# A hand-written order of stages for each engine ahead of the first scan

## What is computed (the reference, cut)

```python
# layer 1: selective scan, 16 states (the part that the change touches)
x_proj = x @ W_xproj.T                       # 64 + 16 + 16 columns: dtp, B, C
dt = softplus(dtp @ W_dt.T + b_dt)           # 256 columns
h = exp(dt * A) * h + dt * B * x             # per time step, feature and state
y = einsum(h, C) + D * x
# layer 2: sign(layernorm(x)*gamma+beta) @ sign(W - mean(W)).T, + bias, * alpha
# layer 3: a second selective scan (rank 128 in place of 64)
# layer 4: mixture of 16 experts, top 2, and 2 shared experts
```

## Time and profile before

| | us |
|---|---|
| median of 3 runs | 688.4 (686.29 to 689.64) |
| profiled execution, its own time | 688.48 |
| its span in the trace | 686.7 |
| PE busy over the span | 623.1 (91%) |
| DVE busy | 528.3 (77%) |
| ACT busy | 503.8 (73%) |
| POOL busy | 419.1 (61%) |

### The profile page before, as it was taken

One profiled execution on the slowest core, in us unless ns is written; L12 is line 12 of the kernel. 1 busy time (PEld: TensorE's weight loads), 2 busy tenths in 40 slices (PEclk: granted clock), 3 DMA queues, 4 the chain that ended last, 5 costly groups with the idle time before them and its releaser, 6 DMA issues.

```text
span 686.7 us, 12401 instructions
## 1 busy us (share of the span) xinstructions
PE 623.1 (91%) x4334; PEld 533.4 (78%) x4337; DVE 528.3 (77%) x900; ACT 503.8 (73%) x1164; POOL 419.1 (61%) x256
## 2 busy tenths in 40 slices
PE   4779999999992778899999999989999999999994
PEld 2369999999992533799999999977677677777673
DVE  6698999999998899799899999967822644444346
ACT  2999999999974866999999999794544562222244
POOL 0037999999999003189999999980774233333400
PEclk9989999999997799999999999999999999999998
DMA  6022454545450000135445544471232233333183
GB/s 192 4 80 89 161 149 146 149 143 155 138 144 0 1 2 5 70 118 156 154 146 154 147 156 144 127 225 42 78 108 100 77 108 106 101 107 107 63 259 123
DMA packets 57575, 77.83 MB, mean 113 GB/s; under 512 B 8112, under 2 KB 38480, under 8 KB 57520
## 3 DMA queue, kind: packets, MB, share of 16 engines
q1 hardware_dynamic: 53728, 66.75, 32.1%
q0 software_dynamic: 3792, 10.36, 4.2%
HBM read 58.21 MB, written 18.87 MB: 112 GB/s over the span
## 4 chain that ended last, share of the span: by engine, by line
PE 64%; DVE 15%; ACT 8%; POOL 8%; issue 3%; DMA 1%; DVEq 0%; ACTq 0%; POOLq 0%
PE both L1311 16%; PE both L1391 12%; PE bank L1340 12%; POOL arena L1118 7%; PE both L1313 5%; PE bank L1399 3%; PE bank L1400 3%; DVE st L411 2%; DVE arena L645 2%; PE bank L1332 2%; PE bank L1493 1%; DVE residual L572 1%; DVE tok_a L497 1%; PE bank L1452 1%; PE bank L1454 1%
## 5 line engine op out<-in xcount | busy, mean ns | idle before, releaser
L1118 POOL TENSOR_TENSOR arena<-arena,rings 128x1024 f32<-128x1024 f32 x126 | 296.6, 2378 | 17.9 <-DVE arena L645 14.0
L1311 PE MATMUL both<-rings,tok_a 128*128 128x128 f32 x1280 | 182.4, 276 | 3.2 <-DVE arena L645 2.8
L1311 PEld LDWEIGHTS both<-rings,tok_a 128*128 128x128 f32 x1280 | 163.8, 192 | 4.7 <-issue 3.5
L645 DVE TENSOR_TENSOR_SCAN arena<-rings,both 128x1024 f32<-128x1024 f32 x64 | 145.3, 2279 | 13.0 <-PE both L1313 7.8
L645 DVE TENSOR_TENSOR_SCAN arena<-late,both 128x1024 f32<-128x1024 f32 x62 | 140.7, 2278 | 6.7 <-PE both L1313 1.5
L1340 PE MATMUL bank<-ident,arena 128*128 128x128 f32 x1024 | 133.0, 273 | 2.8 <-POOL arena L1118 1.4
L1340 PEld LDWEIGHTS bank<-ident,arena 128*128 128x128 f32 x1024 | 115.7, 141 | 4.2 <-POOL arena L1118 1.9
L1003 ACT ACTIVATE rings<-ident,b_tok 128x128 f32<-128x128 f32 x320 | 106.4, 393 | 0.3
L1159 POOL DMA_INDIRECT y_tok<-rings,dest x47 | 45.1, 959 | 84.9 <-DVE rings L798 84.6
L1003 ACT ACTIVATE rings<-tok_a,b_tok 128x256 f32<-128x256 f32 x192 | 89.5, 499 | 0.0
L1313 PE MATMUL both<-ident,rings 128*128 128x128 f32 x384 | 83.9, 273 | 0.0
(11 more groups left out here) (230 smaller groups left out, 976.3 us busy)
## 6 DMA issues: line engine op xcount, KB each, us to landing
rings<-c_rows SPq DMA_DIRECT2D x128, 256.0 KB, 3.4
w_sb<-w SPq DMA_DIRECT2D x18, 352.0 KB, 4.2
x_sorted<-zeros SPq DMA_DIRECT2D x47, 128.0 KB, 3.4
rings<-x_sorted SPq DMA_DIRECT2D x47, 128.0 KB, 2.0
arena<-w SPq DMA_DIRECT2D x2, 2048.0 KB, 12.9
residual<-x SPq DMA_DIRECT2D x4, 512.0 KB, 5.9
tok_a<-y_tok SPq DMA_DIRECT2D x4, 512.0 KB, 7.2
w_sb<-y_tok SPq DMA_DIRECT2D x4, 512.0 KB, 8.0
```

The source lines that it names most:

```text
L645: dve.tensor_tensor_scan(h_s, decay_s.rearrange("p h t -> p (h t)"), both[s % B_RING][:, :], 0.0, ALU.mult, ALU.add).then_inc(h_ready, 1)
L1118: pool.tensor_tensor(h_both, h_both, c_row, ALU.mult).then_inc(hc_ready, 1)
L1311: pe.matmul(o, tok_a[:, c, h * P:(h + 1) * P], v_ring[:, s % V_RING, j, 0:P], start=True, stop=True)
```

## The change

1. Each engine gets its own hand-written list ahead of the first scan: `vector_first`, `scalar_first`, `tensor_first`. GpSimd does its four `dt` products in order, as it did.
2. VectorE takes all four statistics ahead of the norms of batches 1, 2 and 3. The treatment of the second layer's weights (`ffn_weights`) becomes a stage `ffn` behind `err` 1. ScalarE's exponent of `a_sb` becomes a stage `a_exp`.
3. For batches 0 and 1 the maxima are taken by VectorE (stage `relu`, with a semaphore `relu_first`) and not by ScalarE's Relu. TensorE's `pre` 1 and 2 and VectorE's `err` 0 and 1 wait for it.
4. TensorE turns the identity 28 times as soon as the identity has landed, ahead of `turn` 0.
5. `u_turn` 0 stands ahead of `pre` 3 and B's columns on TensorE; the decay factors stand ahead of `log` 3 on ScalarE. `decays` is split in two by name; in `scalar_middle` both stand one behind the other, so nothing moves there.

The rows below are from the programs' lists of instructions: line, operation, output<-inputs, shape, and xN for N in a row. They tell the order, not times.

The diff, without the list of semaphores and with the second half of the lists as they are:

```diff
-        into_ssm = ["x_stat", "x_norm", "turn", "proj", "pre", "err", "log", "b_cols", "dt", "u_turn"]
+        vector_first = [
+            ("x_stat", 0), ("x_norm", 0), ("x_stat", 1), ("x_stat", 2), ("x_stat", 3), ("x_norm", 1), ("x_norm", 2), ("relu", 0),
+            ("err", 0), ("x_norm", 3), ("relu", 1), ("dt", 0), ("err", 1), ("ffn", 0), ("dt", 1), ("err", 2), ("b_cols", 1),
+            ("dt", 2), ("err", 3), ("dt", 3)]
+
+        scalar_first = [
+            ("x_stat", 0), ("turn", 0), ("x_stat", 1), ("x_stat", 2), ("proj", 0), ("x_stat", 3), ("pre", 0), ("turn", 1),
+            ("a_exp", 0), ("proj", 1), ("log", 0), ("turn", 2), ("pre", 1), ("proj", 2), ("turn", 3), ("log", 1), ("pre", 2),
+            ("b_cols", 0), ("proj", 3), ("u_turn", 0), ("log", 2), ("pre", 3), ("decays", 0), ("decays", 1), ("log", 3),
+            ("u_turn", 1), ("u_turn", 2), ("u_turn", 3)]
+
+        tensor_first = [
+            ("turn", 0), ("proj", 0), ("pre", 0), ("turn", 1), ("proj", 1), ("turn", 2), ("pre", 1), ("proj", 2), ("turn", 3),
+            ("pre", 2), ("proj", 3), ("dt", 0), ("u_turn", 0), ("pre", 3), ("b_cols", 1), ("u_turn", 1), ("u_turn", 2)]
...
+                elif name == "ffn":
+                    ffn_weights()
                 elif name == "err":
 
-                    if k == 0:
-                        ffn_weights()
-                    elif k == Q + 2:
+                    if k == Q + 2:
                         keep()
...
                     if l:
                         dve.wait_ge(relu_ready, (q + 1) * H)
+                    elif q < 2:
+                        dve.wait_ge(relu_first, (q + 1) * H)
...
                         dve.tensor_scalar(dtT[:, h, t], bank[2 + h][:, :], bdt_sb[l][:, h:h + 1], 0.0, ALU.add, ALU.max)\
-                           .then_inc(relu_ready, 1)
+                           .then_inc(relu_ready if l else relu_first, 1)
...
-            for name, q in in_turn(into_ssm, range(Q)):
+            for name, q in vector_first:
                 stage(name, q, 0)
...
+                elif name == "a_exp":
+                    for i in range(2):
+                        act.wait_ge(ld_ssm[i], 32)
+                        act.activation(a_sb[i][:, :, :], a_sb[i][:, :, :], ACT.Exp).then_inc(a_exp_ready, 1)
                 elif name == "b_cols":
                     if l == 0 and q == 0:
-                        for i in range(2):
-                            act.wait_ge(ld_ssm[i], 32)
-                            act.activation(a_sb[i][:, :, :], a_sb[i][:, :, :], ACT.Exp).then_inc(a_exp_ready, 1)
                         act.wait_ge(fsign_in, 2)
...
                         act.wait_ge(pre_ready, k * H + h + 1)
-                        if l == 0:
+                        if l == 0 and q >= 2:
                             act.activation(dtT[:, h, t], bank[2 + h][:, :], ACT.Relu, bias=bdt_sb[l][:, h:h + 1])
...
-                    if q == 1 and l == 0:
-                        for s in range(0, ABAR_RING, 2):
-                            decays(l, s)
...
                 elif name == "decays":
-                    for s in range(0, ABAR_RING, 2):
-                        decays(l, s)
+                    decays(l, 2 * q)
...
-            for name, q in in_turn(into_ssm, range(Q)):
+            for name, q in scalar_first:
                 stage(name, q, 0)
...
-            for name, q in in_turn(into_ssm, range(Q)):
-                stage(name, q, 0)
+            for q in range(Q):
+                stage("dt", q, 0)
...
                     if k > Q:
                         pe.wait_ge(relu_ready, q * H)
+                    elif k in (1, 2):
+                        pe.wait_ge(relu_first, k * H)
...
             pe.wait_ge(ld_ident, 16)
-            for name, q in in_turn(into_ssm, range(Q)):
-                if (name, q) != ("u_turn", Q - 1):
-                    stage(name, q, 0)
+            stay_busy(28, bank[4])
+            for name, q in tensor_first:
+                stage(name, q, 0)
```

More of the change, by code:

```diff
@@ L197, in sandwich_kernel @@
         shift_ready, bias_ready, minus_ready = sem("shift_ready"), sem("bias_ready"), sem("minus_ready")
-        g_first, relu_ready = sem("g_first"), sem("relu_ready")
+        g_first, relu_ready, relu_first = sem("g_first"), sem("relu_ready"), sem("relu_first")
         g_normed, x_scaled, rows_normed = sem("g_normed"), sem("x_scaled"), sem("rows_normed")
@@ L255, in sandwich_kernel @@
             ("exp", 0), ("bc", 1), ("turn", 2), ("pre", 1), ("log", 0), ("exp", 1), ("proj", 2), ("turn", 3), ("log", 1), ("bc", 2),
-            ("pre", 2), ("exp", 2), ("proj", 3), ("log", 2), ("bc", 3), ("pre", 3), ("u_turn", 0), ("exp", 3), ("decays", 1),
+            ("pre", 2), ("exp", 2), ("proj", 3), ("log", 2), ("bc", 3), ("pre", 3), ("u_turn", 0), ("exp", 3), ("decays", 0), ("decays", 1),
             ("log", 3), ("u_turn", 1), ("u_turn", 2), ("u_turn", 3)]
@@ L1538, in diagonals @@
     return 2 if 1 <= batch_state(s)[1] <= 2 * CQ else 3
-def in_turn(stages, batches=range(Q - 1, -1, -1)):
-    for step in range(len(stages) + Q - 1):
-        for q in batches:
-            if 0 <= step - q < len(stages):
-                yield stages[step - q], q
 class Tile:
```

## The result

| us | before | after |
|---|---|---|
| median, beside each other on one chip | 689.02 (4 runs, 686.29 to 691.25) | 695.74 (4 runs, 693.06 to 700.36) |
| profiled execution; its span | 688.48; 686.7 | 694.72; 692.9 |
| ScalarE's first input part | 49.64 | 52.99 |
| first scan step of VectorE | 53.17 | 58.06 |
| first scan step to the last of the first scan | 154.34 | 154.35 |

What follows compares the result with a forecast made beforehand. Bound: ScalarE, almost gapless from `pre` 0 to the first input part at 49.64. Terms -3.65 - 2.3 + 0.96 + 5.35 = +0.35, then +1.5 + 0.93 for the clock, gave +2.8: 691.2 us, 8 in 10 for 687.0 to 693.6.

Steps and rivals of the forecast that it cites:

- `pre` 0 at 15.7: First stretch: with statistics ahead of norms and 28 turns, `pre` 0 starts at 15.7, not 19.34: -3.65 us.
- Rival 3: Start of TensorE: the 28 turns don't raise the clock, `pre` 0 from 18, 2.2 later; 693.4 us, chance 0.08.
- ScalarE's new waits: ScalarE from `pre` 0 to the input part: waits sum to 6.7 us against 1.35 before, +5.35.
- The 0.25 at the signs: ScalarE at the signs of the weights, 34.6: TensorE's turn and the hand-overs cost 0.25 us.
- the 0.3 in `pre` 0: ScalarE's first wait, between the two halves of `pre` 0: 0.3 us.
- Rival 1: `pre` 0 to input part: 32.5 us, as tight as between the layers; input part 48.2, 687.0 us, chance 0.16.
- The prediction's two bounds for the waits: ScalarE's waits behind 15.7: under 6.3 us the tight order decides; under 3.5, input part 46.2, gain over 0.5%.
- VectorE held by GpSimd at w: `err` 1 on VectorE: its w meets GpSimd's `dt` product, +1.05 us, or nothing if VectorE goes first.
- The clock's term: TensorE's low clock after gaps 30.7 to 35.4 (+1.5, bounds 0 and 2.4) and 44.5 to 49.4 (+0.93, 0 and 1.9).
- What stands behind that runs as before: Behind the first input part, 49.64: nothing changes, so a microsecond there is a microsecond at the end.
- Rival 2: TensorE's two new gaps: the clock stays high through both, +0.35 us in all; 688.8 us, chance 0.16.
- The marks that it named: Signs in the trace: `pre` 0 about 15.7, waits at `proj` 1, `log` 1, `pre` 3, 22 turns nearly 3.9, input part 51 to 52.5.

Runs made afterwards that it cites:

- e2: The changed kernel without the 28 turns of the identity at the start; 699.25 us, 1.0102 of the kernel before.
- e1: The changed kernel with 15, 38 and 42 turns of the identity in TensorE's three gaps; 689.83 us, 1.0013 of the kernel before.
- e4: The changed kernel with `err` 1 ahead of `dt` 0 and `err` 2 ahead of `dt` 1 on VectorE; 691.54 us, 1.0012 of the kernel before.
- f2: The changed kernel with norm 1 ahead of statistics 3 on VectorE, `turn` 1 ahead of `pre` 0 on ScalarE and TensorE; 700.38 us, 1.0068 of before.
- g4: The changed kernel measured once more, unaltered; 693.88 us, 1.0102 of the kernel before.
- g1_stats_row: The kernel before with only VectorE's statistics of batches 1 to 3 ahead of their norms; 687.18 us, 0.9991 of the kernel before.
- f1_before_28: The kernel before with 28 turns of the identity at its start and nothing else; 696.4 us, 1.0006 of the kernel before.
- g3_third_gap: The changed kernel with 42 turns of the identity behind `u_turn` 1, in the third gap alone; 691.1 us, 1.0036 of the kernel before.
- g2: The changed kernel with reordered lists, 20 and 14 turns behind `u_turn` 0 and 1, and 34 more between the layers; 683.92 us, 0.9919 of before.
- f3: The changed kernel with the order of e4 and 15, 20 and 42 turns of the identity in TensorE's gaps; 696.25 us, 1.0007 of the kernel before.
- the second set: Second of three sets of follow-up runs, on one chip beside the kernel before (median 695.29 us there); f1_before_28, f2 and f3 belong to it.

## Why the prediction was wrong

It had the sign, and a time of 691.2 with a range up to 693.6; the measured 695.74 lies outside. At the first scan step it had +2.78 (0.35, 1.5 and 0.93), and the trace has +4.89. Of the 4.5 us between 691.2 and 695.74 these are 2.1, which alone would give 693.3, still in the range; 1.3 came behind the first scan step, 0.6 because the kernel before measured 689.02 and not 688.4 this time, and 0.5 lie between spans and medians. By its own steps:

- *`pre` 0 at 15.7.* 16.05. The 28 turns took 5.57, past the 5 us of its high end; the clock rose in them and `proj` 0 took 1.93. Rival 3 did not come, and e2 shows how it would have looked (`pre` 0 at 17.75 without the turns; it had 18). The Trainium skill, "TensorE: Matmul & The Clock Gate", section "What's actually happening", has activity release the high level; `turn` 0 at 1.04 with the turns and 1.94 without agrees.
- *ScalarE's new waits, +5.35 and with them +0.35 in all.* Right in place, and nearly in size. With the clock held high (e1) they are 1.88 (2.0 predicted), 2.52 (2.6), 0.73 (0.55) and 0.79 (1.0), and the first scan step stands 0.45 behind that of before. The 0.25 at the signs and the 0.3 in `pre` 0 did not come. e4 and f2 take single waits away, and each moves part of its time to a later wait.
- *Rival 1, the new order as tight as between the layers* (32.5 us from `pre` 0 to the input part). It took 36.9, and 33.8 in e1 with the clock high, where the waits behind `pre` 0 sum to 5.9: so 3.1 of the 4.4 us to this rival were the clock's. The prediction's two bounds for the waits don't fit its own sum, in which the input part is at 43.3 plus the waits: 48.2 needs 4.9 and not 6.3, and 46.2 needs 2.9 and not 3.5.
- *VectorE held by GpSimd at w.* Right: three of three, 1.82 to 1.84 for two.
- *The clock's term, 1.5 + 0.93 = 2.43: this is the step that failed.* Held against e1_awake it cost 4.64 in both profiled executions of the changed kernel. In the first, the gap of 1.86 us ahead of `proj` 1 counted too, 1.54, where the prediction listed two gaps only, "30.7 to 35.4 and [...] about 44.5 to 49.4"; its own words on the earlier trace rows ("gaps of 2 us and weak work") had room for it, since by its own times TensorE, done with `turn` 1, stands idle for ScalarE's Exp and copies up to 19.2. The two it listed cost 1.56 (1.5 predicted) and 1.54 (0.93): the third stretch lasted 6.83 us, into the first products of the scan, where the one between the layers, from which the 0.93 was taken, lasted 3.4 in the kernel before. In the second (g4) the gap at `proj` 1 cost nothing and the listed ones 2.65 and 2.00, both above their bounds of 2.4 and 1.9. So a missing gap is one way in which the term was too small, and too low a price for the listed ones the other; the 22 turns, forecast at nearly 3.9, took 3.13 and 4.23. For the first execution the difference to the forecast at the first scan step, 4.89 - 2.78 = 2.11, is 1.54 for the stretch left out, 0.06 and 0.61 for the other two, 0.35 for `pre` 0, and 0.45 less for the waits.
- *"What stands behind that runs as before."* The scan does (154.34 and 154.35). Between the layers 1.18 more went. No line there was changed, and the same code took from 83.53 (g1_stats_row) to 85.06 (f1_before_28) in two kernels that keep the old lists there and ahead of it nearly so. Both executions of the changed kernel lie high (84.84; 82.09 with the shorter meeting told last, so 84.95 without), but g3_third_gap, with the same lists, has 80.59 with that meeting, so 83.45 without. So the executions alone spread as widely, and a share of the change in it isn't shown. The last 0.5 us between 6.2 (spans) and 6.7 (medians) stays open.

Rival 2, the clock that stays high, was given 688.8 at 0.16: e1_awake is that case, at 1.0013 of the kernel before. It was the right number for a kernel that the change did not make. The range's upper end, 693.6, already lay above the sum with both of the clock's bounds (0.35 + 2.4 + 1.9, so 693.1); what it had no place for were a clock's term of 4.64, and 1.2 us more between the layers. The marks that it named came out so: the waits at `proj` 1 (3.42 for 2.0), `log` 1 and `pre` 3 were in place, the input part at 52.99 lay just past its 51 to 52.5.

## What to carry to other kernels

Here each new wait of ScalarE stood close to an idle time of the engine that it waited for, and when that was TensorE the idle time had a second price, the low clock on the work behind it: 4.64 us for three gaps of 1.9 to 4.8, the single ones 0 to 2.65. So list TensorE's idle times out of the new order first, all of them, and price the sum; turns of the identity in them brought the time back to that of before (1.0116 to 1.0013). The list is no sure guide to where the clock falls. Behind the gap of 4.8 us ahead of `u_turn` 2 it was low in all six profiles in which the gap was left open. Behind the gap of 1.86 at `proj` 1 it fell in two executions (the first measurement and g3) and not in two others (e4 and g4), and in f2 and g2 it fell with no gap over 1.2 us ahead of it since the start of the work. And an early start moves the end only if the other engines' lists let it through: the statistics alone, or the 28 turns alone, gave nothing that the time shows (0.9991 and 1.0006).

## What the runs showed of the hardware

One meeting of VectorE and GpSimd, in code that no kernel here touches (the norm behind the first scan, beside GpSimd's addition to the residual), has two outcomes. VectorE's timeline, changed kernel, first measurement:

```profile
222.59 5.53 DVE L572 TENSOR_SCALAR tok_a<-residual,mom,rstd 128x256 f32<-128x256 f32 x4
```

The same line of the same program in g4_after_again:

```profile
223.28 2.67 DVE L572 TENSOR_SCALAR tok_a<-residual,mom,rstd 128x256 f32<-128x256 f32 x4
```

In the kernel before it was 5.53. Of the 14 profiled executions nine had 5.53 and five 2.66 or 2.67 (f2, f3, g2, g3 and g4), and no other value came. It moves the second scan by 2.9 us, about as much as the change was predicted to cost. The Trainium skill, "SBUF — State Buffer", section "Who interferes with whom", says that a VectorE operation in a two-port mode, which a `tensor_scalar` can take, and a GpSimd operation shut each other out, whoever issues first. The trace agrees: the same four operations take 1.38 us where GpSimd is idle, and GpSimd's sixteen additions take 10.94 us where VectorE needs 5.53 and 11.14 where it needs 2.67. It also shows that how often VectorE is held is not fixed by the program. What tips it isn't shown; a comparison of single profiles should look at this row first.

In the second set, the part behind the second scan took 8 to 11 us longer in every kernel's profile, with a low stretch of the clock at about 512 to 530, which none of the other profiles has but that of e1_awake (there at 463 to 484). The kernel before has no profile in that set, but its median was some 6 us higher too (695.29).
